# Grouped attention layers: one maximum ahead of the sixth pair of scores, and the first half of the shift copied ahead of two exponentials

## What is computed

```python
def _L1_xattn_ref(x, cond, wq, wk, wv, wo, norm_w):   # 16 heads of 32, 4 key/value heads
    residual = x
    xn = rmsnorm(x, norm_w)
    q = (xn @ wq).reshape(B, T, N_HEADS, HEAD_DIM)
    k = (cond @ wk).reshape(B, S, N_KV_HEADS, HEAD_DIM)
    v = (cond @ wv).reshape(B, S, N_KV_HEADS, HEAD_DIM)
    qg = q.reshape(B, T, N_KV_HEADS, n_rep, HEAD_DIM)
    scores = jnp.einsum('btgrd,bsgd->bgrts', qg, k) * scale
    attn = jax.nn.softmax(scores.astype(jnp.float32), axis=-1).astype(q.dtype)
    out = jnp.einsum('bgrts,bsgd->btgrd', attn, v).reshape(B, T, N_HEADS * HEAD_DIM)
    return residual + out @ wo
```

## Time and profile before

| what | value |
|---|---|
| three executions | 4169.87, 4171.4, 4172.85 us; median 4171.4 us |
| the profiled execution | 4174.46 us, of which 4172.7 us are its span |
| PE busy | 4045.4 us, 97% of the span |
| DVE, ACT, POOL busy | 59%, 50%, 48% |
| mean granted clock of PE | 0.987 |
| turns, first to last (the grouped layers) | 2163.9 to 4134.1 us |

### The profile page before, as it was taken

The page is one execution under the profiler, slowest core; times in us unless marked ns, Lnnn a source line. Parts: engine busy times, 40 slices in busy tenths (PEclk is TensorE's granted clock), DMA queues, the critical chain, the costliest instruction groups (busy, mean ns, idle before and its releaser), DMA issues. The chain is left out here.

```text
span 4172.7 us, 52197 instructions
## 1 busy us (share of the span) xinstructions
PE 4045.4 (97%) x19446; PEld 2632.7 (63%) x19446; DVE 2452.1 (59%) x3456; ACT 2085.0 (50%) x2659; POOL 2004.8 (48%) x1072
## 2 busy tenths in 40 slices
PE   9999999998999999999969999999999999999999
PEld 7888888885566665666534555555555555555555
DVE  3122300013665566655567788778777887788775
ACT  3111211122444445444446666666766676667665
POOL 0000000002555557555626766676667666666666
PEclk9999999998999999999979999999999999999999
DMA  5333522233545555454332333333333333333322
GB/s 184 134 131 133 175 84 86 82 104 105 139 131 136 135 135 140 130 135 126 91 90 80 85 86 96 87 96 95 95 86 86 86 108 96 86 86 96 89 76 66
DMA packets 312790, 447.00 MB, mean 107 GB/s; under 512 B 44728, under 2 KB 116408, under 8 KB 312552
## 3 DMA queue, kind: packets, MB, share of 16 engines
q1 hardware_dynamic: 312552, 443.84, 37.9%
HBM read 215.07 MB, written 102.77 MB: 76 GB/s over the span
## 5 line engine op out<-in xcount | busy, mean ns | idle before, releaser
L1902 DVE TENSOR_REDUCE a_max_cols<-a_ps 128x1 f32<-128x512 f32 x1536 | 1018.1, 673 | 326.0 <-PE a_ps L2034 319.9
L1795 ACT ACTIVATE a_probs<-a_ps 128x1024 f32<-128x1024 f32 x768 | 784.6, 1025 | 606.8 <-PE a_ps L2065 601.5
L2034 PE MATMUL a_ps<-a_k_ops,a_q_ops 96*128 96x512 f32 x1536 | 653.2, 437 | 50.2 <-DVE a_max_cols L1902 33.2
L1704 POOL TENSOR_TENSOR a_sums<-a_probs 128x1024 f32<-128x1024 f32 x192 | 456.0, 2390 | 321.9 <-ACT a_probs L1795 320.7
L2034 PEld LDWEIGHTS a_ps<-a_k_ops,a_q_ops 96*128 96x128 f32 x1536 | 291.8, 190 | 397.6 <-DVE a_max_cols L1902 220.1
L1043 DVE TENSOR_REDUCE a_max_cols<-a_ps 128x1 f32<-128x512 f32 x512 | 340.7, 687 | 289.4 <-PE a_ps L1206 289.3
L2065 PE MATMUL a_ps<-a_q_ops,a_k_ops 128*128 128x512 f32 x1536 | 493.7, 403 | 1.5 <-ACT a_q_ops L1786 0.9
L807 POOL MEMSET a_ident<- 128x128 f32 x1 | 0.2, 204 | 974.9 <-issue 974.9
L1704 POOL TENSOR_TENSOR a_sums<-a_sums,a_probs 128x1024 f32<-128x1024 f32 x192 | 454.0, 2385 | 0.0
L2079 PE MATMUL a_ps<-a_probs,a_v 128*32 128x512 f32 x3072 | 411.3, 607 | 0.9 <-ACT a_probs L1795 0.9
L303 DVE TENSOR_TENSOR cp_c_lo<-cp_raw,cp_c_hi 128x1024 fp32r<-128x1024 f32 x64 | 78.4, 1226 | 527.7 <-ACT cp_c_hi L247 527.6
(11 more groups left out here) (139 smaller groups left out, 7429.8 us busy)
## 6 DMA issues: line engine op xcount, KB each, us to landing
a_k_ops<-k_scratch SPq DMA_DIRECT2D x192, 256.0 KB, 4.5
a_q_ops<-a_qn_hi SPq DMA_DIRECT2D x768, 64.0 KB, 2.0
k_scratch<-cp_out SPq DMA_DIRECT2D x88, 512.0 KB, 2.8
cp_raw<-in_ctx_t SPq DMA_DIRECT2D x64, 512.0 KB, 4.0
a_q_ops<-a_qn_hi SPq DMA_DIRECT2D x256, 128.0 KB, 2.3
x_raw<-out_t SPq DMA_DIRECT2D x25, 1024.0 KB, 7.1
a_q_ops<-a_qn_lo SPq DMA_DIRECT2D x384, 64.0 KB, 2.0
a_x_res<-out_t SPq DMA_DIRECT2D x92, 256.0 KB, 3.1
```

The lines of the kernel that those rows point to most:

```text
L1704: pool.tensor_tensor(sums[:, hp], (probs if n < H else sums)[:, hp], probs[:, n], ALU.add)\
L1795: act.activation(probs[:, n], ps[:, 2 * (n % 2):2 * (n % 2) + 2, :], ACT.Exp).then_inc(exped, 1)
L1902: dve.tensor_reduce(max_cols[:, t % 2, col:col + 1], bank(b), AX.X, ALU.max, negate=True)\
L2034: pe.matmul(bank(b), q_ops[0:SHIFT, s, h, q * P:(q + 1) * P], k_ops[0:SHIFT, s, :], start=True, stop=True).then_inc(smax, 1)
```

## The change

Two calls change places, each with its neighbour, in the lists of ACT and PE of `grouped_layers`. On ACT, the first half of the shift for tile t+1 is copied ahead of exponential 6, and not between exponentials 6 and 7. On PE, `maximum` 12 stands ahead of `scores` 6, and not behind it.

```diff
@@ act, batch
-                    exponential(it, t, 6)
                     if there(it, t + 1):
                         shift(*at(it, t + 1), 0)
+                    exponential(it, t, 6)
                     exponential(it, t, 7)
                     if there(it, t + 1):
                         shift(*at(it, t + 1), 1)
@@ pe, batch
                     turn(*at(it, t + 1))
+                    maximum(it, t, 12)
                     scores(it, t, 6)
-                    maximum(it, t, 12)
                     maximum(it, t, 13)
                     scores(it, t, 7)
```

## The result

The changed kernel takes 4135.9 us (median of 6 executions, 4135.4 to 4139.69) against 4171.15 us for the kernel before (6 executions): a ratio of 0.9917, 95% interval 0.9906 to 0.9928. It is 35 us faster. The forecast was 4128 us, 43 us faster. In a second run, on the chip of the last experiments, it took 4135.8 us, 0.9916 of before (0.9903 to 0.9930).

The account below looks back on a forecast made before the run. The prediction took PE to set the pace, with stalls at tile ends, and DVE's chain to bound t = 0 tiles. 32.7 + 10.1 = 42.8 us less than 4171.4 gave 4128.6, say 4128 us; range 4111 to 4150.

Parts of the forecast that it names:

- PE's stalls in the tiles with t > 0: End of these tiles: three held PE steps lose 0.46 us a tile and would go, 71 x 0.46 = 32.7 us.
- 0.24, 0.11 and 0.11: Losses in us: scores 7 to maximum 14, 0.24; maximum 14 to outputs 2, 0.11; last outputs to denominators, 0.11.
- ACT's chain: Tiles with t > 0: half the shift, exponentials 6 and 7, other half; ends 0.18 us before PE's denominators.
- The cover of exponential 6: Tiles with t > 0: it starts 0.76 us later, yet ends 0.63 before PE wants scores 0's banks; cost nothing.
- The t = 0 tiles: DVE's chain starts earlier there, so PE's maximum 0 comes 0.42 us earlier; 24 x 0.42 = 10.1 us.
- Subtraction 0, not stretched: On DVE in t = 0 tiles: issued earlier, it takes 0.68 us and ends at 3008.44.
- The rule that the prediction set against the change: Trainium skill: two-input DVE instruction and SBUF-reading GpSimd instruction contend; the first keeps the port throughout. Term: 24 x 0.29 to 0.42.
- its lower bound: T = 0 tiles: subtraction 1 takes its full 0.68 us behind POOL's multiplication, so maximum 0 comes 0.29 earlier.
- The rival that the t = 0 tiles give PE's full pace: Maximum 0 comes 1.08 us earlier in t = 0 tiles, 24 x 1.08 = 25.9 us; 4113 us, chance 0.08.
- the rivals: Others: shift stays the gate, 4144 us, chance 0.17; gain given back later in tile, 4171, 0.07; slower, 4187, 0.04.

Follow-up runs that it names:

- e1: The kernel before with only PE's half of the change (maximum 12 ahead of scores 6): 4191.1 us, ratio 1.0045.
- e2: The kernel before with only ACT's half of the change (first half of the shift ahead of exponential 6): 4159.0 us, ratio 0.9972.
- e5: The changed kernel with the second half of the shift also ahead of exponentials 6 and 7: 4197.8 us, ratio to before 1.0060.
- e4: The changed kernel with POOL's last sum and multiplication in t = 0 tiles cut from 512 columns to 8: 4113.05 us, ratio to before 0.9856.
- e8: The changed kernel with only POOL's last sum in t = 0 tiles cut to 8 columns: 4129.4 us, ratio 0.9900.
- e7: The changed kernel with DVE's four subtractions moved further, 2 and 3 behind the reduce of the next tile's maximum 0: 4111.5 us, ratio 0.9858.
- e3: The changed kernel with DVE's three subtractions in t = 0 tiles each moved behind the next reduce: 4132.8 us, ratio 0.9903.
- e6: The kernel before with DVE's three subtractions in t = 0 tiles each moved behind the next reduce: 4165.2 us, ratio 0.9983.

## Why the prediction was right, and where it was off

- **PE's stalls in the tiles with t > 0** were the right term: 0.24, 0.11 and 0.11 were forecast to go, and all three did. 0.46 a tile was forecast and 0.48 to 0.49 came; the little more is that the step behind the denominators' first matmuls also fell, from 0.88 to 0.86. In the traces this is 33.4 us where 32.7 were forecast, and another 1.8 come from the tiles with t = 0, nearly all from the one of batch 1, which had 3.4 us at the lower clock before and has none now. The forecast doesn't count these 1.8, and no run shows that the change brings them: as far as is known they are luck.
- **ACT's chain** ran by the forecast to 0.02 us: copies 0.69 behind the turn's start (0.70), denominators at 5.25 (5.24 or 5.25). That PE's half loses without ACT's follows from the forecast's steps, though it doesn't say so; e1 and e2 show it.
- **The cover of exponential 6** was real and a little smaller than stated: e5 shows 0.50 where the forecast had 0.63, counted up to the end of exponential 6; scores 0 starts 0.15 behind that end in e5. The change needed none of it.
- **The t = 0 tiles**, 24 x 0.42 = 10.1 us, are the step that failed; they gave nothing, and without them the forecast would have been about 4139 us. The range of 4111 to 4150 held the time all the same: it is 39 us wide, and this term is 10. "Subtraction 0, not stretched" was wrong. The prediction took its 0.79 for nearly plain length and let POOL's part begin with the multiplication at 3008.40, because that was the row with a long duration. The instruction ahead of it on POOL, the last sum, ran until 3008.45 and had held subtraction 0 already before the change. So it ended 0.56 after that sum in both kernels, however early it was issued. The rule that the prediction set against the change was right, and applied to that sum too it gives a gain of 0, below the 0.29 of its lower bound. e4 and e8 show that it was POOL. The term's count was also 2 too high: batch 0 has no multiplication in its tile with t = 0, and batch 23 no subtractions.
- The rival that the t = 0 tiles give PE's full pace, 1.08 us, had the right price, but the change doesn't bring it: e7 gets 1.07 of it (5.11 to 4.04) by moving the subtractions, and another 0.11 in the step behind maximum 0, so that the tile is 1.19 shorter from turn to turn.
- None of the rivals came about.

## What to carry to other kernels

When two engines share a resource, an instruction that is issued earlier isn't finished earlier as long as the other engine holds it. Count from the end of what is running on the other engine, and read the row ahead of the long one too. If a chain of one engine bounds a tile, an edit that feeds it later loses, even where it frees another engine; find the edit that starts the chain sooner and make both. And an instruction that can be held belongs behind the ones that the pacing engine is waiting for.

## What the runs showed of the hardware

- A DVE subtraction with two inputs in SBUF against POOL instructions that read SBUF: 0.68 us alone; with POOL first it ends 0.54 to 0.56 us after POOL's end, whatever it waited. In the rows above it is 0.56 and 0.55 after the sum, 0.56, 0.55 and 0.54 after the multiplication in e8, e3 and e7, and 0.55 in the changed kernel's subtraction 1; in the traces of the kernel before, the changed kernel and all experiments, the ends of POOL and of all 355 subtractions held in the tiles with t = 0 lie 0.54 to 0.56 apart. DVE's reduces from PSUM took 0.68 or 0.69 in all rows shown of t = 0 tiles, beside POOL's instructions throughout.
- POOL's multiplication, issued while a subtraction was waiting, let it go first: it took 1.73 and not 1.28 in the changed kernel, and its last 1.28 us begin at 2990.20, near the subtraction's end at 2990.35. That it stood aside in between is read from these two numbers and not shown by a run of its own.
- A matmul of `maximum` that had to wait costs PE about 0.11 us beyond the wait, in the step to the `outputs` behind it: 0.44 against 0.33.
- TensorE's granted clock went to its lower level (0.50) for 3.4 us at a time inside the grouped layers, at a cost of 1.2 to 1.5 us each. Each of the falls told above came near the end of a wait of PE of 1.3 to 2.6 us or within 2 us behind it (e5's 1.31, the kernel before's 2.57), but waits as long also passed without one (2.60 in e2 and in e7, 1.91 in e6). Traces of one kernel and another differ by them, so a difference of a few us between two traces has to be looked up in the granted clock first.
